# Last layer of a four-layer recurrent block: wide projections behind the first pair of score blocks, row norms two sequences ahead, one scan and half of the decays moved

## The reference

```python
u, z = split(xn @ in_proj.T)                   # 256 channels each
x = silu(causal_conv4(u)); dbl = x @ x_proj.T  # 64 time-step + 16 B + 16 C columns
delta = softplus(softplus(dbl[:64] @ dt_proj.T + b) + b)
state = exp(delta * A) * state + delta * x * B      # 16 states, scanned over 256 rows
s = ((sum_n state * C + x * D) * silu(z)) @ out_proj.T
q, k, v = rope(xn @ Wqkv + b); attn = softmax(q k / sqrt(8)) @ v   # 16 heads of 8
x1 = layernorm(xn + attn @ Wo); route x1 to 2 of 8 experts; h = gelu(x1 @ W1[e]) @ W2[e]
z = layernorm(x1 + sum_e weight_e * h_e)
```

## Time and profile before

| | |
|---|---|
| median of 3 runs | 2924.54 us |
| profiled execution, its own time / its span | 2924.43 / 2922.4 us |
| mean granted TensorE clock | 0.857 |
| PE busy, share of the span | 2500.6 us, 86% |
| DVE busy | 2324.8 us, 80% |
| ACT busy | 1689.2 us, 58% |
| POOL busy | 339.3 us, 12% |

### The profile page before, as it was taken

The page is one execution under the profiler, slowest core; times in us unless marked ns, Lnnn a source line. Parts: engine busy times, 40 slices in busy tenths (PEclk is TensorE's granted clock), DMA queues, the critical chain, the costliest instruction groups (busy, mean ns, idle before and its releaser), DMA issues. The chain is left out here.

```text
span 2922.4 us, 55768 instructions
## 1 busy us (share of the span) xinstructions
PE 2500.6 (86%) x18940; PEld 1895.1 (65%) x18940; DVE 2324.8 (80%) x6071; ACT 1689.2 (58%) x3432; POOL 339.3 (12%) x368
## 2 busy tenths in 40 slices
PE   1899999899999999877858988888898888888886
PEld 0666666677777777665836665666665666666565
DVE  1899999788877888676267888888888888888887
ACT  1677777465665665544355656565565655565654
POOL 0000000000000000034411111111111111111111
PEclk9999999899999999988858877678876778877777
DMA  9000000000000000020223433334342334343334
GB/s 245 2 0 0 0 0 0 1 2 1 0 1 0 1 0 1 5 81 17 67 76 95 109 93 75 86 90 105 99 102 76 84 81 109 95 107 84 78 89 109
DMA packets 89593, 165.43 MB, mean 57 GB/s; under 512 B 18728, under 2 KB 48688, under 8 KB 89392
## 3 DMA queue, kind: packets, MB, share of 16 engines
q0 software_dynamic: 20480, 62.94, 11.3%
q1 hardware_dynamic: 65600, 98.77, 10.8%
q10 hardware_dynamic: 3312, 1.32, 0.2%
HBM read 92.61 MB, written 11.67 MB: 36 GB/s over the span
## 5 line engine op out<-in xcount | busy, mean ns | idle before, releaser
L1141 ACT ACTIVATE b_neg<-b_neg,b_nmax 128x128 f32<-128x128 f32 (+1 forms) x512 | 190.9, 443 | 206.6 <-DVE b_nmax L1295 206.6
L2557 ACT ACTIVATE d_probs<-l_bank,w_b 128x256 f32<-128x256 f32 x512 | 210.8, 469 | 155.6 <-PE l_bank L2396 153.3
L2807 DVE TENSOR_TENSOR_SCAN d_state<-w,d_state 128x1024 f32<-128x1024 f32 x128 | 291.0, 2284 | 3.8 <-issue 3.4
L2396 PE MATMUL l_bank<-xnT,w_w 128*128 128x256 f32 x1024 | 245.1, 382 | 14.8 <-ACT d_probs L2557 14.8
L2407 PE MATMUL l_bank<-w_w,d_probs 128*128 128x128 f32 x2048 | 252.7, 276 | 0.0
L2407 PEld LDWEIGHTS l_bank<-w_w,d_probs 128*128 128x128 f32 x2048 | 244.9, 192 | 11.7 <-ACT d_probs L2557 5.3
L2337 PE MATMUL l_bank<-w 9*128 9x256 f32 x1040 | 208.7, 669 | 26.1 <-ACT w L2481 18.9
L2520 ACT ACTIVATE w<-d_delta,w_A_log 128x255 f32<-128x255 f32 x520 | 220.1, 498 | 0.0
L94 POOL TENSOR_TENSOR ln_rstd<-ln_var_eps,minus_half 128x2 f32<-128x2 f32 x51 | 70.5, 1383 | 1280.1 <-DVE ln_var_eps L88 1280.1
L2396 PEld LDWEIGHTS l_bank<-xnT,w_w 128*128 128x128 f32 x1024 | 184.7, 190 | 41.5 <-ACT d_probs L2557 21.7
L2337 PEld LDWEIGHTS l_bank<-w 9*128 9x128 f32 x1040 | 123.5, 320 | 96.8 <-issue 31.5
(11 more groups left out here) (406 smaller groups left out, 5704.1 us busy)
## 6 DMA issues: line engine op xcount, KB each, us to landing
d_bct<-l_bc SPq DMA_DIRECT2D x132, 512.0 KB, 4.0
d_state<-d_state POOLq DMA_DIRECT2D x96, 512.0 KB, 6.6
d_state<-d_state POOLq DMA_DIRECT2D x32, 256.0 KB, 4.1
x_sorted<-x SPq DMA_DIRECT2D x1, 2580.0 KB, 24.7
y_rows<-x SPq DMA_DIRECT2D x1, 2112.0 KB, 24.5
c2e_xg<-x_sorted SPq DMA_DIRECT2D x16, 129.0 KB, 2.2
w<-in_L_ffn_w_dram SPq DMA_DIRECT2D x1, 2048.0 KB, 9.5
w_w<-in_L_ffn_W_dram SPq DMA_DIRECT2D x1, 2048.0 KB
```

The costliest lines, as they stand in the source:

```text
L1141: done = nc.scalar.activation(neg[:, slot, cols], neg[:, slot, cols], ACT.Exp, bias=nmax[:, slot, a:a + 1], scale=-1.0)
L2396: done = nc.tensor.matmul(bank[:, b, i * T:(i + 1) * T], w.w1[:, e, k * P:(k + 1) * P], x1T[:, :], start=True, stop=True)
L2557: done = v.activation(hid[:, e % 2, k, :], bank[:, b, i * T:(i + 1) * T], ACT.Gelu, bias=w.b1[:, e, k:k + 1])
L2807: done = v.tensor_tensor_scan(group, dA[i][:, g % (NG - 1), :, :].rearrange("p m t -> p (m t)"), group, 0.0, ALU.mult, ALU.add)
```

## The change

PE, ACT, DVE and POOL get new orders in the last layer; no instruction's shape changes.

- `project_uz` is split into `project_u(0)`, `project_u(1)` and `project_z`. `project_u(0)` of the sequence after goes behind `scoresT(0)`, ahead of `out_rows`, and `scoresT(1)` and `exp_scores(1)` go behind `out_rows`. `project_u(1)` goes behind `scoresT(3)`, `project_z` behind `scoresT(5)`. They write banks 4 and 5; the transposes of the normed rows, of y and of x1 go to bank 2 and the products behind them to bank 3. `down(0)` and `down(1)` now wait for the activations that empty banks 4 and 5.
- Rows are normed two sequences ahead, among the experts: `norm_stats(n + 2)` behind `times_c(2)`, `norm_rows` behind `times_c(3)`, the transposes behind the bias product of `down(6)`, the copy on ACT ahead of `log_part(0)`. The transposes of k wait for it.
- DVE's scan (1,1) goes from the pairs stage behind `route_shift`, where (2,0) was, and `times_c(1)` and scan (2,0) go among the `add_expert` calls; `first_part` goes behind `rotate(1)`, ahead of `add_expert(7)`.
- The decays of state groups 0 and 1 (four of eight sets) are computed ahead of `copy_qm`; for it the second softplus sum goes behind the first `heads_max`.
- POOL: the power of n + 2 goes between `add_group(2)` and `add_group(3)`, and `add_group(1)` behind `residual`.

```diff
@@ TensorE, attention_front(n)
                 pe.wait_ge(dt_taken, n + 1)
+                pe.wait_ge(xnT_ready, n + 2)
                 turn_heads(1, bank[:, 2:4, :]).then_inc(kT_in_psum, 1)
...
-                for p in range(2):
-                    scoresT(n, p)
+                scoresT(n, 0)
+                project_u(0)
@@ TensorE, loop
                         if k % 2 == 0:
                             heads_out(k // 2 - 1)
+                        if k == 3:
+                            project_u(1)
                         if k == 5:
-                            turn_x(n + 1, 1 - par)
+                            project_z()
...
                     done.then_inc(o_in_psum, 1)
-                    project_uz()
                     qkv_rows(1)
...
                             done.then_inc(b2_in_psum, 1)
+                            turn_x(n + 2, par)
                     attention_front(n + 1)
                     out_rows(n)
+                    scoresT(n + 1, 1)
@@ ScalarE
                              scale=float(HD3) ** -0.5).then_inc(probs_ready, 1)
-                decays(n, p // 2, p % 2)
+                if p % 2:
+                    decays(n, 2 + p // 4, p // 2 % 2)
...
+                    copy_xnT(n + 2)
                     log_part(n + 1, 0)
                     copy_qk(n + 1)
                     log_part(n + 1, 1)
+                    for k in range(4):
+                        decays(n + 1, k // 2, k % 2)
                     copy_qm(n + 1)
@@ VectorE, loop
-                    norm_stats(nc, c, s, n + 1)
                     scan(0, 0)
-                    norm_rows(n + 1, 1 - par)
                     scan(0, 1)
                     times_c(0)
                     scan(1, 0)
-                    scan(1, 1)
-                    times_c(1)
                     dve.wait_ge(o_turned, n + 1)
...
-                    scan(2, 0)
+                    scan(1, 1)
                     route_best(nc, r, n)
...
                     add_expert(0)
+                    times_c(1)
+                    scan(2, 0)
+                    add_expert(1)
                     scan(2, 1)
+                    add_expert(2)
                     times_c(2)
-                    add_expert(1)
+                    norm_stats(nc, c, s, n + 2)
+                    add_expert(3)
                     scan(3, 0)
-                    add_expert(2)
+                    add_expert(4)
                     scan(3, 1)
                     times_c(3)
-                    add_expert(3)
+                    norm_rows(n + 2, par)
+                    add_expert(5)
                     take_qkv(n + 1, 1)
                     rotate(0)
-                    add_expert(4)
+                    add_expert(6)
                     rotate(1)
                     v.drain()
-                    add_expert(5)
                     first_part(n + 1)
-                    add_expert(6)
                     add_expert(7)
...
                     for blk in range(NBLK):
                         heads_max(n + 1, blk)
+                        if blk == 0:
+                            softplus_sum(n + 1, 1)
@@ GpSimd, loop
-                    norm_power(nc, c, s, n + 1)
-                    add_group(1)
                     inner_power(2 * n + 1)
                     residual(n + 1, 1 - par)
+                    add_group(1)
                     add_group(2)
+                    norm_power(nc, c, s, n + 2)
                     add_group(3)
```

More of the change, by code:

```diff
@@ L2273, in qkv_rows, with project_u, project_z @@
                     .then_inc(qkv_in_psum, 1)
-            def project_uz():
-                for i in range(CI):
-                    for k in range(DCONV):
-                        done = nc.tensor.matmul(bank[:, 2, i * T:(i + 1) * T], u_projT[:, i, k, :], xpad[:, k:k + T],
-                                                start=(k == 0), stop=(k == DCONV - 1))
-                done.then_inc(u_in_psum, 1)
-                for i in range(CI):
-                    done = nc.tensor.matmul(bank[:, 3, i * T:(i + 1) * T], z_projT[:, i, :], xnT,
+            def project_u(i):
+                for k in range(DCONV):
+                    done = nc.tensor.matmul(bank[:, 4, i * T:(i + 1) * T], u_projT[:, i, k, :], xpad[:, k:k + T],
+                                            start=(k == 0), stop=(k == DCONV - 1))
+                if i == CI - 1:
+                    done.then_inc(u_in_psum, 1)
+            def project_z():
+                for i in range(CI):
+                    done = nc.tensor.matmul(bank[:, 5, i * T:(i + 1) * T], z_projT[:, i, :], xnT,
                                             start=True, stop=True)
@@ L2294, in project_dt @@
                 pe.wait_ge(xdbl_ready, m + 1)
-                pe.wait_ge(zg_ready, m + 1)
+                if later(m):
+                    pe.wait_ge(logits_taken, m)
                 for i in range(CI):
@@ L2367, in _ @@
                 qkv_rows(a)
-            project_uz()
+            for i in range(CI):
+                project_u(i)
+            project_z()
             project_x(0, 0)
             project_dt(0)
+            turn_x(1, 1)
             attention_front(0)
+            scoresT(0, 1)
             with pe.Fori(0, NSEQ // 4) as m:
@@ L2477, in copy_xnT @@
                 act.wait_ge(s.xnT_in_psum, m + 1)
-                v.activation(xnT, bank[:, 5, 0:T], ACT.Copy).then_inc(xnT_ready, 1)
+                v.activation(xnT, bank[:, 2, 0:T], ACT.Copy).then_inc(xnT_ready, 1)
             def copy_q(banks):
@@ L2492, in silu_uz @@
                 for i in range(CI):
-                    done = v.activation(xs[:, par, i, :], bank[:, 2, i * T:(i + 1) * T], ACT.Silu,
+                    done = v.activation(xs[:, par, i, :], bank[:, 4, i * T:(i + 1) * T], ACT.Silu,
                                         bias=w.conv_b[:, i:i + 1])
@@ L2496, in silu_uz @@
                 act.wait_ge(z_in_psum, m + 1)
-                v.activation(zg[:, par, :, :].rearrange("p i t -> p (i t)"), bank[:, 3, :], ACT.Silu)\
+                v.activation(zg[:, par, :, :].rearrange("p i t -> p (i t)"), bank[:, 5, :], ACT.Silu)\
                     .then_inc(zg_ready, 1)
@@ L2540, in _ @@
             copy_xdbl(0)
+            copy_xnT(1)
             log_part(0, 0)
@@ L2543, in _ @@
             log_part(0, 1)
+            for k in range(4):
+                decays(0, k // 2, k % 2)
             copy_qm(0)
@@ L2590, in _ @@
                     v.activation(th_z[:, :, :], rows[:, :, :], ACT.Tanh, scale=0.5).then_inc(th_z_ready, 1)
-                    for p in range(2):
-                        exp_scores(n + 1, p)
+                    exp_scores(n + 1, 0)
                     act.wait_ge(s_in_psum, n + 1)
@@ L2595, in _ @@
                         .then_inc(s_taken, 1)
+                    exp_scores(n + 1, 1)
         @block.gpsimd
@@ L2693, in _ @@
             norm_rows(0, 0)
+            norm_stats(nc, c, s, 1)
             dve.wait_ge(a_exp, 1)
@@ L2790, in _ @@
                 v.drain()
+            norm_rows(1, 1)
             first_part(0)
```

31 lines of the change are left out of this document (16 added, 15 removed).

## The result

The changed kernel takes 3107.73 us (median of 4 runs, 3101.22 to 3126.09), the kernel before 2924.62 beside it (4 runs, 2924.23 to 2925.05). The ratio is 1.0637, 95% interval 1.0615 to 1.0659: slower, as forecast, and far more so (183 us where 48 were forecast). It is inside the range, near its upper end. The profiled execution took 3105.0 us, 180.6 above that of before.

A forecast was written before the change was run, and what follows sets the result against it. PE was taken to bound the experts, DVE the scores, and PE, ACT and DVE together the pairs. 4.3 + 1.3 - 2.7 = 2.9 us a turn, 46 in 16, plus about 2 at the end, gave 2972 us; range 2900 to 3115.

The forecast's parts named there:

- the cold start: Start of experts: without u and z before it, first wide work runs at half rate; 1.3 us late, bounds 0 and 4.
- the pairs: Pairs stage: PE's work adds up to 25.9 us against 28.6 before, 2.7 us less in a turn.
- From there at full clock: Pairs, after project_u(0) and out_rows (10.1 us): the remaining PE work runs at half its former durations, stage 25.9 us.
- the first rival: Clock stays low in the pairs: some 36 us with one short full-clock stretch, about 3135 us in all sequences; chance 0.17.
- In some of the sequences only: Pairs: the clock stays low in only part of the sequences, total about 3050 us; chance 0.13.
- The rule on keeping TensorE busy: Pairs: a skill page says continuously busy TensorE gets the full clock; the forecast noted 24.80 of 28.59 us busy at 0.50.
- Experts and scores: DVE's added work and later first_part make scores end 4.3 us late, bounds 3.5 and 5; cold start adds 1.3.
- Decays ahead: Scores: four decay sets, 6.4 us, hide in ACT's 9.71 us wait; ACT would then allow pairs in some 22 us.
- Rows: Rows stage: losing u and z costs nothing on the path, since DVE's chain is busy through the stage.
- Ends: End of the kernel: the last out_rows stands behind a project_u(0), adding about 2 us.
- Waits of DVE: Signs: none before the last two add_expert, first maximum about 7 us after first_part's dneg, turned-output wait over 2.27 us.
- The third rival: Pairs go at ACT's pace with early full clock and warm experts: -2.6 us a turn, about 2883 us; chance 0.12.

The follow-up runs named there:

- experiment 5: Changed kernel with project_u(0) computed twice, the second writing the same values: 3098.1 us, ratio 1.0609.
- 9: Kernel of experiment 6 with ten wide matmuls, whose product nothing reads, added in the pairs stage: 2958.05 us, ratio 1.0134.
- experiment 1: Changed kernel with u and z computed in the rows stage again, scoresT(0) and (1) together: 2986.09 us, ratio 1.022.
- experiment 4: Kernel before with only the decays of groups 0 and 1 ahead, softplus sum behind the first maximum: 2929.6 us, ratio 1.0028.
- Experiments 6: Changed kernel keeping only norm two ahead and decays ahead; u, z, scans, rotations and first_part at their old places: 2912.32 us, ratio 0.9968.
- experiment 8: Kernel before with the norm two ahead alone, all decays in the pairs: 2910.96 us, ratio 0.9962.
- experiments 7: Norm and decays ahead as in experiment 6, but u and z in the pairs stage as in the changed kernel: 3045.28 us, ratio 1.0426.
- 11: Kernel of experiment 7 with u and z spread evenly over the pairs stage, both first score blocks together: 2993.64 us, ratio 1.0245.
- experiment 2: Changed kernel with scan (1,1) and times_c(1) back in the pairs stage, scan (2,0) back behind route_shift: 3087.53 us, ratio 1.0602.

## Why the prediction was right or wrong

**Direction: right. Bound: in part.** The kernel is slower, and DVE's order and the cold start cost time as forecast. But the pairs, forecast as 2.7 us gained, lose 4.0, though their mean clock rose from 0.50 to 0.66: the wide work moved there costs more than the clock gives back.

**The failed step: "From there at full clock".** The prediction let the clock rise in `project_u(0)` and `out_rows` and stay up to the end of the pairs, as the wide pieces come every few microseconds. The rise comes at that place in all 15 turns. It stays in 2 of them, and there the stage takes 26.2 and 26.3 us, near what was worked out (25.9). In thirteen it falls again after 3.4 us, `project_u(1)` is paid at half rate in all of these and z in eight; six turns take 37, near the 36 of the first rival. The mean is 33.0: +4.0 where -2.7 was forecast, 6.7 of the 8.6 us by which each turn was missed. What the rows and runs show in its place: in most turns a wide piece buys a few microseconds of full clock, not a stage. Added pieces lengthen these stretches (clock 0.66 to 0.75 in experiment 5, 0.50 to 0.69 in 9), and no version held 1.00. Of the forecast cases the outcome is the second of rival 1, "In some of the sequences only", but its time of about 3050 was too low: in most turns the clock is down for more of the stage than it is up.

**The rule on keeping TensorE busy.** PE was busy 32.88 of 36.95 us at 0.55 and 21.90 of 26.23 at 0.83: 89% and 83%, with the lower clock in the busier turn. The Trainium skill, "TensorE: Matmul & The Clock Gate", section "Why this matters for your kernels", would have TensorE kept continuously busy for the full clock. This trace, like the earlier trace rows, doesn't agree: the busy share doesn't tell which clock is granted, and in the earlier trace rows PE works from 2123.38 to 2131.54 without a wait, all of it at half rate. That page's rule carried neither the sum nor the choice of its fast side. What carried them was the rise at 2154.08 behind full-width work, and that row showed where the clock rises, not how long it stays up once narrow work follows.

**Experts and scores: right in kind, too small.** 5.6 us forecast with the cold start, 7.1 measured. The cold start was taken at 1.3, between bounds of 0 and 4, and is 1.3 (experiment 1); that the choice hit so closely is luck. The rest was taken at 4.3 and is 5.8. Most of that miss is in the added DVE work, taken at 6.4 us against 3.0 of waits. The first `add_expert` of the turn of the earlier trace rows:

```profile
2081.53 0.61 DVE L2825 SCALAR_TENSOR_TENSOR same_head<-l_bank,until,d_x 128x128 f32<-128x128 f32 x2 [0.68 <-PE l_bank L2407]
```

From its start to the end of the last one it took 2107.32 - 2081.53 = 25.79 us before, 22.77 without the two waits of the earlier trace rows; after, 2184.93 - 2154.84 = 30.09, with no such wait left. So the added work is 7.3 us in this turn (7.4 in the mean of 15), some of it in short gaps of 0.2 us ahead of the added steps, and the last `add_expert` ends 4.3 late where 3.3 were forecast. From there to the first maximum it takes 4.7 us (2189.66 - 2184.93), the upper end of the 4.0 to 4.7 that were worked out; in the mean of experiment 1 it is 4.5, 0.6 more than before, where the sum had 0.2. The softplus sum was taken at 0.77 and costs 0.83 (experiment 4). Of the 5.8 us, 4.7 are the order of rotations, `first_part` and scan.

**Decays ahead: hidden, as forecast.** ACT's wait shrank from 9.71 to 2.52. They don't help either: ACT's order was said to set the pace of the pairs with PE just behind it, and PE was so close behind that 6.4 us less for ACT gained 0.3 (experiment 4).

**Rows: 0 forecast, 0.4 measured.** Before, the clock rose in this stage and stayed up; after, it rises for 3.4 to 6.9 us and falls again (mean 0.67). PE now waits where u and z stood, and the small matmuls behind the wait run at half rate: the transposes of x1 take 0.69 us, 0.38 before.

```profile
2144.38 0.69 PE L2450 MATMUL l_bank<-ident,d_x 128*128 128x128 f32 x2 [3.55 <-DVE d_x L2788]
```

**POOL and SP: 0 forecast, and no cost shows.** Experiments 6 and 8 keep POOL's new order and are faster than the kernel before.

**Ends: 2 forecast, 2.0 measured.** The forecast counted 16 turns, the mean above 15, so most of the 8.6 us left over is the sixteenth turn. Its rows, experts and scores are 7.6 us longer (11.57 + 37.02 + 16.45 against 11.25 + 32.43 + 13.80), what follows them to the end of the span is 2.0 longer (24.62 against 22.62), and the first rows stage begins 0.8 earlier.

**Waits of DVE:** none in front of the last two `add_expert`, 6.2 us from the dneg of `first_part` to the first maximum (about 7 forecast), and 14.8 us for the turned output where more than 2.27 was. These signs held.

**The third rival** (faster, warm pairs) fails at its first condition: even in the best turns the transposes of q (1.97 us) and nearly all of `project_u(0)` (3.51) run at half rate. One part in the change's favour wasn't priced by itself: the prediction counted the norm among the experts as 1.6 us of DVE work, and norm ahead alone gains 0.38% (experiment 8).

## What to carry to other kernels

Before wide matmuls are moved between narrow ones to lift the clock, count them at both clocks: here they cost 5.7 us in a turn, and the clock they bought held for only part of the stage. Leave wide work where it keeps the next full-rate stage warm, and spread it if it must move (52 us between experiments 7 and 11). On an in-order engine, work fits for free only ahead of a wait; whatever the next stage needs first (here rotations and `first_part`) keeps its early place, and an added scan is tested together with the place of what it pushes.

## What the runs showed of the hardware

- The granted clock rose in or at the end of a piece of 5.6 us of full-width matmuls in all 15 turns. In thirteen it fell 3.4 us later under 9-row and 32-column matmuls, in two it stayed up for 17.1 us with the same instructions: a stage of 26.2 us with PE busy for 83% of it, against one of 37.0 with 89%.
- With such a clock a kernel's time scatters: 3101 to 3126 us in 4 runs of the changed kernel and 3079 to 3118 in experiment 2, against 2924.2 to 2925.1 before and 2984.8 to 2986.9 with the wide work out of the pairs.
- Four more full-width matmuls in each turn made no measurable difference (experiment 5, 3098.1 against 3107.7): the mean clock of the pairs was higher, 0.75 against 0.66.
- What decides whether the clock holds in a given turn isn't settled by these runs. The two turns shown differ ahead of the fall only in where the rise comes: within `project_u(0)` (3.51 us) or behind `out_rows` (3.78, then 1.91). That place goes with the outcome: in the 45 turns of the changed kernel and experiments 2 and 7, whose PE order in the pairs is the same, the clock rose up to 8.4 us after the start of the stage in eleven turns and stayed up for 17 us in eight of them; it rose later in 34 and fell after 3.4 us in every one. An early rise isn't enough. In this turn of the changed kernel it came as early as in the fast one, PE then waited 2.01 us, and the next score block is slow:

```profile
1911.92 3.52 PE L2277 MATMUL l_bank<-d_xpad,w_u_projT 128*128 128x256 f32 x8
1915.28 1.05 PE L2349 MATMUL l_bank<-w_out_projT,d_ym 128*128 128x128 f32 x8
1916.26 1.13 PE L2340 MATMUL l_bank<-w 9*128 9x256 f32 x8
1919.40 2.08 PE L2340 MATMUL l_bank<-w 9*128 9x256 f32 x8 [2.01 <-ACT d_probs L2540]
```
